# A scatter chain on GpSimd: an expert's output rows are issued when those of the expert one place ahead have landed

## The chip, the cores and the metric

The kernel runs on one core of a Trainium2 chip. The metric is the device time of one execution in microseconds (us), given as the median of several executions. Its engines are named as the profile names them: PE is TensorE (PEld its weight loads), DVE is VectorE, ACT is ScalarE, POOL is GpSimd, SP is SyncE. A DMA is issued by an engine and then moves its bytes on the core's 16 DMA engines; when all 16 have reported, a semaphore has risen by 16 and the DMA has landed.

## The reference

A decoder block on x of shape (16, 256, 256), three parts, each added to the running x after a layer norm: a selective state-space scan, a dynamic time warping alignment with a second input, and a mixture of experts. The change touches only the last one:

```
gate_logits = x @ gate_kernel                      # 4096 tokens, 64 experts
weights, selected = top_k(gate_logits, 2); weights = softmax(weights)
per expert: out = (silu(xe @ w0[e]) * (xe @ w1[e])) @ wo[e]      # 256 -> 512 -> 256
y[token] = sum over its 2 experts of weight * out
```

So each of 4096 tokens has two rows of expert output, 8192 rows of 256 floats (1 KB) in all, and y is their weighted sum.

## The kernel before, in words

The kernel is written in direct instructions, one program for each engine, with semaphores between them. Four stages follow each other: the scan (to about 510 us), the time warping (to about 720 us), the stage `expand` that applies the alignment, makes the normalized tokens `xn`, routes them and clears the DRAM array `outs` to zero (to about 837 us), and the stage `experts` (lines 2130 to 2493), in which everything below happens.

`outs` in DRAM has one row for each (token, choice) pair and after them a region of rows into which unused places of a tile are dumped. `K.table` lists for each place of an expert the token row to fetch, `K.choice` the row of `outs` to write. Experts are ranked by their number of tokens, and each rank has a fixed room: the 32 largest have 220 down to 134 rows ("wide", two tiles of at most 128 rows), the others 128 rows ("narrow", one tile). `TURN` takes 63 ranks alternately, a wide one at even places k and a narrow one at odd k. What doesn't fit in the rooms, and the 64th rank, is worked off afterwards in a loop over "late" tiles whose number is read at run time; with these inputs it runs once.

For each place k in 0..62:

- SP loads the expert's weights (1.5 MB, three DMAs of 512 KB, `load_weights`, issue line 2127) into a ring of 4; the load for place k waits until place k-4 has left the ring (`down_mm`).
- POOL fetches the token rows with indirect DMAs, one per tile (`gather`, line 2221), into `mo_xg`, a ring of XR = 4 buffers. The gather of place k+4 waits until PE has turned the tile of place k (`turned`).
- PE transposes the rows (`turn`, line 2274; DVE copies them to `mo_xt` at line 2411), multiplies with w0 and w1 (`up`, line 2288), ACT takes the silu (line 2370), DVE the product (line 2417), PE multiplies with wo (`down` line 2294 for narrow, `down_wide` line 2302 and the turning back `back` line 2313 for wide ones).
- DVE copies the result to `mo_o`, a ring of XR = 4 buffers (`take_out`, line 2428), and raises `o_ok`. Before it does, it waits for the landing of the scatter four places ahead, which used the same buffer (`o_out[k % XR]`).
- POOL sends the rows to `outs` with indirect DMAs that add to what lies there (`scatter`, line 2228), one per tile; each raises `o_out[k % XR]` by 16 when it has landed. `moved(k)` is the value that this semaphore has once place k and all before it in the same buffer have landed.

POOL's program is written out in this order:

```
for k in range(RANKS):
    if k + XR < RANKS:
        gather(k + XR)
...
    scatter(k)
```

After the 63 places POOL's late loop (from line 2246) scatters the late tile (line 2250, a plain write), fetches the next one and prepares its indices. Then SP waits for all `o_out`, reads `outs` back in 16 DMAs of 512 KB (line 2209), DVE forms the weighted sums (line 2491), and ACT sends them out.

Of the kernel before, what the change touches and what calls it, by code (L numbers as in the profile page):

```python
# [44 lines left out]
RANKS = E - 1  # L45
# [29 lines left out]
def settle(eng):  # L75


    eng.nop(nofuse=True)
# [80 lines left out]
XR = 4  # L159
# [1970 lines left out]
def experts(K):  # L2130
# [3 lines left out]
    with ExitStack() as c:  # L2134
# [25 lines left out]
        o_out = [sem(f"mo_o_out{u}") for u in range(XR)]  # L2160
# [17 lines left out]
        moved = lambda k: sum(16 * len(tiles(j)) for j in range(k % XR, k + 1, XR))  # L2178
# [5 lines left out]
        def late_count(eng):  # L2184
            return eng.value_load(K.late_n[0:1, 0:1], min_val=1, max_val=LATE + 1)  # L2185

        @block.sync
        def _(sp):
            sp.wait_ge(x_in[0], moved(0))
            for k in range(1, WRING):  # L2190
                load_weights(K, sp, expert_at(K, sp, k), k)
            for k in range(WRING, RANKS):
                sp.wait_ge(down_mm, (k - WRING + 1) * FC)
                load_weights(K, sp, expert_at(K, sp, k), k % WRING)
            n = late_count(sp)
            with sp.Fori(0, n) as g:
                e = sp.value_load(K.late_of[0:1, bass.ds(g, 1)], min_val=0, max_val=E - 1)
                sp.wait_ge(done, g + 1)
                settle(sp)
                load_weights(K, sp, e, RANKS % WRING)  # L2200
            for u in range(XR):
                if u != LAST:
                    sp.wait_ge(o_out[u], moved_by(u))
            sp.wait_ge(o_out[LAST], n * 16 + moved_by(LAST))
            settle(sp)
            for k in range(TT // G):
                if k >= GOT:
                    sp.wait_ge(added, (k - GOT + 1) * 2 * G)
                sp.dma_start(got[k % GOT][:, :, :, :],
                             K.outs_dram[2 * k * G * P:2 * (k + 1) * G * P, :].rearrange("(t p i) d -> p t i d", p=P,  # L2210
                                                                                       i=2)
                             ).then_inc(got_in[k % GOT], 16)

        @block.gpsimd
        def _(pool):

            def gather(k):
                if k >= XR:
                    pool.wait_ge(turned, k - XR + 1)
                for a, at, n in tiles(k):  # L2220
                    nc.gpsimd.indirect_dma_start(xg[k % XR][0:n, a, :], None, K.xn_dram[:, :],  # L2221
                                                 bass.IndirectOffsetOnAxis(ap=K.table[0:n, at:at + 1], axis=0)
                                                 ).then_inc(x_in[k % XR], 16)

            def scatter(k):
                pool.wait_ge(o_ok, k + 1)
                for a, at, n in tiles(k):
                    nc.gpsimd.indirect_dma_start(K.outs_dram[:, :],  # L2228
                                                 bass.IndirectOffsetOnAxis(ap=K.choice[0:n, at:at + 1], axis=0),
                                                 o_sb[k % XR][0:n, a, :], None,  # L2230
                                                 compute_op=ALU.add).then_inc(o_out[k % XR], 16)

            for k in range(1, XR):
                gather(k)
# [3 lines that stand above are left out]
                if k + XR == RANKS:  # L2238
                    nc.gpsimd.tensor_copy(to[:, :], K.choice[:, LATE0:LATE0 + 1]).then_inc(indices, 1)
                    pool.wait_ge(turned, RANKS - XR + 1)  # L2240
                    nc.gpsimd.indirect_dma_start(xg[LAST][:, 0, :], None, K.xn_dram[:, :],
                                                 bass.IndirectOffsetOnAxis(ap=K.table[:, LATE0:LATE0 + 1], axis=0)
                                                 ).then_inc(x_in[LAST], 16)
                scatter(k)
            n = late_count(pool)
            with pool.Fori(0, n) as g:
                pool.wait_ge(o_ok, g + RANKS + 1)
                pool.wait_ge(indices, g + 1)
                settle(pool)
                nc.gpsimd.indirect_dma_start(K.outs_dram[:, :], bass.IndirectOffsetOnAxis(ap=to[:, :], axis=0),  # L2250
                                             o_sb[LAST][:, 0, :], None).then_inc(o_out[LAST], 16)
                pool.wait_ge(named_ok, g * 3 + 3)
                settle(pool)
                nc.gpsimd.indirect_dma_start(xg[LAST][:, 0, :], None, K.xn_dram[:, :],
                                             bass.IndirectOffsetOnAxis(ap=index[:, :], axis=0)).then_inc(x_in[LAST], 16)
                pool.wait_ge(x_in[LAST], g * 16 + (moved_by(LAST) + 32))
                pool.wait_ge(o_out[LAST], g * 16 + (moved_by(LAST) + 16))
                settle(pool)
                nc.gpsimd.tensor_copy(to[:, :], to_next[:, :]).then_inc(indices, 1)
            for u in range(XR):  # L2260
                if u != LAST:
                    pool.wait_ge(o_out[u], moved_by(u))
            settle(pool)

        @block.tensor
        def _(pe):
# [40 lines left out]
            def back(k):  # L2307
                pe.wait_ge(ot_ok, backs(k))
                if k >= 2:
                    pe.wait_ge(o_ok, k - 1)  # L2310
                for a, _, n in tiles(k):
                    for c_ in range(DC):
                        m = nc.tensor.transpose(o_ps[k % 2][0:n, a, c_ * P:(c_ + 1) * P],  # L2313
                                                ot[:, c_, a * P:a * P + n], K.ident[:, :])
                m.then_inc(back_mm, 1)
# [89 lines left out]
        def _(dve):  # L2405
# [14 lines left out]
            def take_out(k):  # L2420
                if wide[k]:
                    dve.wait_ge(back_mm, backs(k))
                else:
                    dve.wait_ge(down_mm, k * FC + FC)
                if k >= XR:
                    dve.wait_ge(o_out[k % XR], moved(k - XR))
                for a, _, n in tiles(k):
                    m = nc.vector.tensor_copy(o_sb[k % XR][0:n, a, :], o_ps[k % 2][0:n, a, :])  # L2428
                m.then_inc(o_ok, 1)
# [172 lines left out]
```

## Time and profile before

| | us |
|---|---|
| median of 3 executions | 1307.4 (1305.8 to 1307.7) |
| the profiled execution, its own time | 1307.59 |
| its span, first to last instruction | 1305.8 |
| stage `experts`, first gather to last scatter issue | 837.3 to 1258.4 |
| from there to the end (late tile, read back, sums) | 1258.4 to 1305.8 |
| PE busy in the span | 1036.5 (79%) |
| POOL busy in the span | 695.1 (53%) |

The profiled execution stands 0.2 us above the median, and its span 1.8 us below its own time. The profile consists of a page (busy time by engine, the span cut in 40 slices, DMA queues, the chain that ended last, groups of instructions) and of views of the trace for stretches of it: instructions in order of time, who waited for whom, busy time in a stretch, and DMA traffic by queue in a stretch. Queue q1 is that of SP and carries the weights, q0 is that of POOL and carries gathers and scatters. POOL's "busy" for a DMA is the time in which it writes the descriptors; the bytes move later.

### The profile page before, as it was taken

The numbers are of one execution on the slowest core, as the hardware profiler recorded it, in microseconds if no ns is written. First come the engines' busy times: TensorE is split into PE (matmuls) and PEld (weight loads), VectorE is DVE, ScalarE is ACT, GpSimd is POOL, SyncE is SP. The second block draws the span as 40 slices with busy tenths as digits, with TensorE's granted clock in tenths as the row PEclk, the third lists the DMA queues.
The fourth block names the chain that finished last, engine by engine and source line by source line (L and its number), as shares of the span: only waits on it lengthen the run. The fifth ranks groups of instructions, "written<-read, shape, count | busy, mean of one in ns | idle before, by whom it ended". The sixth has DMA issues, their size and how long they took to land. (4 is left out here: it accounts for less than half of the span.)

```text
span 1305.8 us, 21090 instructions
## 1 busy us (share of the span) xinstructions
PE 1036.5 (79%) x6867; PEld 924.2 (71%) x6867; DVE 927.7 (71%) x2072; ACT 580.2 (44%) x1286; POOL 695.1 (53%) x609
## 2 busy tenths in 40 slices
PE   5767888787878768477746788799999999999970
PEld 4666767686767757466511576599999999999960
DVE  6999999999999996688798599433333333333348
ACT  3768787878778764344340454121221222222210
POOL 4886868788888870200000554346556565655620
PEclk8889989999999999555578899599999999999985
DMA  8644555464646551122203244499999999999939
GB/s 241 191 142 143 162 164 176 135 203 140 190 150 199 158 168 42 26 41 49 41 1 129 89 149 151 167 291 277 267 271 281 292 288 303 295 306 298 278 105 351
DMA packets 177597, 239.82 MB, mean 184 GB/s; under 512 B 33778, under 2 KB 104486, under 8 KB 176848
## 3 DMA queue, kind: packets, MB, share of 16 engines
q1 hardware_dynamic: 153968, 215.06, 52.1%
q0 software_dynamic: 17184, 18.97, 7.0%
q10 hardware_dynamic: 6336, 4.44, 1.1%
q8 instruction: 55, 0.90, 0.3%
q14 instruction: 54, 0.44, 0.1%
HBM read 203.01 MB, written 31.19 MB: 179 GB/s over the span
## 5 line engine op out<-in xcount | busy, mean ns | idle before, releaser
L1010 PE MATMUL st_y_ps<-ident,st_hc 128*128 128x128 f32 x2048 | 273.6, 292 | 113.3 <-DVE st_hc L529 113.2
L1010 PEld LDWEIGHTS st_y_ps<-ident,st_hc 128*128 128x128 f32 x2048 | 255.4, 203 | 135.6 <-DVE st_hc L529 134.7
L412 POOL TENSOR_TENSOR st_u<-st_dx,codes 128x1024 f32<-128x1024 f32 x127 | 296.4, 2361 | 39.2 <-DVE st_h L521 31.4
L521 DVE TENSOR_TENSOR_SCAN st_h<-st_da,st_u 128x512 f32<-128x512 f32 x256 | 297.6, 1203 | 0.2 <-POOL st_u L412 0.2
L2288 PE MATMUL mo_h<-mo_xt,w 128*128 128x128 f32 (+17 forms) x2048 | 282.1, 289 | 2.0 <-DVE mo_xt L2411 2.0
L2288 PEld LDWEIGHTS mo_h<-mo_xt,w 128*128 128x128 f32 x2048 | 271.6, 193 | 6.6 <-issue 2.7
L2417 DVE TENSOR_TENSOR mo_inter<-mo_silu,mo_h 128x128 f32<-128x128 f32 (+17 forms) x256 | 77.8, 304 | 246.2 <-ACT mo_silu L2370 204.3
L2228 POOL DMA_INDIRECT outs<-mo_o,choice x95 | 149.6, 1575 | 149.2 <-DVE mo_o L2428 130.3
L2370 ACT ACTIVATE mo_silu<-mo_h 128x128 f32<-128x128 f32 (+17 forms) x256 | 74.4, 291 | 286.6 <-PE mo_h L2288 198.5
L748 ACT ACTIVATE st_da<-st_delta,st_a_neg 128x510 f32<-128x510 f32 x256 | 172.1, 685 | 58.6 <-DVE st_h L521 54.1
L529 DVE TENSOR_TENSOR st_hc<-st_h,st_cps 128x1024 f32<-128x1024 f32 x128 | 152.5, 1192 | 0.0
L2221 POOL DMA_INDIRECT mo_xg<-xn,table x93 | 92.7, 997 | 33.7 <-issue 28.1
L1294 PE MATMUL wv_e<-wv_r,wv_shift 128*128 128x1 f32 x274 | 75.9, 348 | 40.3 <-DVE wv_r L1232 39.4
L1294 PEld LDWEIGHTS wv_e<-wv_r,wv_shift 128*128 128x128 f32 x274 | 68.5, 312 | 48.0 <-issue 46.0
L755 ACT ACTIVATE st_cps<-codes 128x512 f32<-128x512 f32 x128 | 76.7, 599 | 43.4 <-DVE st_hc L529 42.1
L2302 PE MATMUL mo_ot_ps<-mo_inter,wo 128*128 128x190 f32 (+16 forms) x512 | 84.7, 298 | 0.0
L1652 POOL TENSOR_SCALAR ex_on<-ex_apart,ex_reach 128x256 f32<-128x256 f32 x32 | 30.3, 959 | 97.1 <-ACT ex_apart L1980 97.0
L2294 PE MATMUL mo_o_ps<-wo,mo_inter 128*128 128x256 f32 x256 | 74.2, 393 | 0.4 <-DVE mo_inter L2417 0.4
L2302 PEld LDWEIGHTS mo_ot_ps<-mo_inter,wo 128*128 128x128 f32 x512 | 73.6, 190 | 0.0
L1284 ACT ACTIVATE wv_r<-wv_e,wv_edge_big 128x1 f32<-128x1 f32 x137 | 35.8, 261 | 64.6 <-PE wv_e L1294 64.6
L1363 POOL MEMSET ex_earlier<- 128x128 bf16 x1 | 0.2, 205 | 104.8 <-POOLq L1107 104.8
L1232 DVE TENSOR_TENSOR_SCAN wv_r<-wv_m,wv_r,wave 128x64 f32<-128x64 f32 x136 | 47.8, 352 | 4.8
(394 smaller groups left out, 1472.9 us busy)
## 6 DMA issues: line engine op xcount, KB each, us to landing
codes<-bc SPq DMA_DIRECT2D x256, 256.0 KB, 3.7
w<-in_L_ffn_w_dram SPq DMA_DIRECT2D x128, 512.0 KB
wo<-in_L_ffn_wo_dram SPq DMA_DIRECT2D x64, 512.0 KB
outs<-ex_zero SPq DMA_DIRECT2D x16, 512.0 KB, 3.2
co_got<-outs SPq DMA_DIRECT2D x16, 512.0 KB, 6.0
wave<-dist SPq DMA_DIRECT2D x16, 274.0 KB
x<-in_x_dram SPq DMA_DIRECT2D x8, 512.0 KB, 9.4
st_cx<-in_ctx_dram SPq DMA_DIRECT2D x8, 512.0 KB, 4.0
```

The lines of the kernel that those rows point to most:

```text
L412: nc.gpsimd.tensor_tensor(u_sb[k % URING][:, :, :], dx[p % 2][:, :, :], over_chunks(b_sb[k % BRING]), ALU.mult).then_inc(u_ok, 1)
L521: nc.vector.tensor_tensor_scan(h_sb[k % HRING][:, dh, :], da_ps[dh][:, :], u_sb[k % URING][:, dh, :], 0.0, ALU.mult, ALU.add).then_inc(h_o ...
L529: nc.vector.tensor_tensor(hc_sb[k % RING][:, :, :], h_sb[k % HRING][:, :, :], over_chunks(c_ps[k % 2][:, :]), ALU.mult).then_inc(hc_ok, 1)
L748: nc.scalar.activation(by_batch(da_ps[dh][:, :]), by_batch(delta[p % 2][:, dh, :]), ACT.Exp, scale=a_neg[:, dh, n:n + 1]).then_inc(da_ok, 1)
L755: nc.scalar.activation(c_ps[k % 2][:, :], c_sb[k % CRING], ACT.Copy).then_inc(c_ok, 1)
L1010: m = nc.tensor.matmul(y_ps[t // 2][:, t % 2, dh * P:(dh + 1) * P], hc_sb[k % RING][:, dh, t * P:(t + 1) * P], K.ident[:, :], start=False, ...
L1294: nc.tensor.matmul(e_ps[t % 4][:, 0:1], K.shift[:, :], r[:, t + 1, SW:SW + 1], start=True, stop=True).then_inc(e_mm, 1)
L2221: nc.gpsimd.indirect_dma_start(xg[k % XR][0:n, a, :], None, K.xn_dram[:, :], bass.IndirectOffsetOnAxis(ap=K.table[0:n, at:at + 1], axis=0) ...
L2228: nc.gpsimd.indirect_dma_start(K.outs_dram[:, :], bass.IndirectOffsetOnAxis(ap=K.choice[0:n, at:at + 1], axis=0), o_sb[k % XR][0:n, a, :], ...
L2288: ins = nc.tensor.matmul(h_ps[m][:, i, 0:n], K.w[r][i][:, c_, m * P:(m + 1) * P], xt[u][:, c_, 0:n], start=(c_ == 0), stop=(c_ == DC - 1))
L2302: ins = nc.tensor.matmul(ot_ps[:, c_, 0:n], K.w[r][2][:, m, c_ * P:(c_ + 1) * P], inter[m][:, 0:n], start=(m == 0 and c_ == 0), stop=(m == ...
L2417: nc.vector.tensor_tensor(inter[m][:, 0:n], silu[m][:, 0:n], h_ps[m][:, 1, 0:n], ALU.mult).then_inc(inter_ok, 1)
```

## The change

`scatter(k)` gets a second wait: for k of 1 and more, POOL waits until all tiles of place k-1 have landed, before it issues the tiles of place k. The late loop's scatter waits for the landing of the last place, 62, as well. No instruction, transfer or buffer is added, removed or resized; the order of POOL's instructions stays.

```
             def scatter(k):
                 pool.wait_ge(o_ok, k + 1)
+                if k >= 1:
+                    pool.wait_ge(o_out[(k - 1) % XR], moved(k - 1))
                 for a, at, n in tiles(k):
                     nc.gpsimd.indirect_dma_start(K.outs_dram[:, :],
...
             with pool.Fori(0, n) as g:
                 pool.wait_ge(o_ok, g + RANKS + 1)
                 pool.wait_ge(indices, g + 1)
+                pool.wait_ge(o_out[(RANKS - 1) % XR], moved(RANKS - 1))
                 settle(pool)
```

How POOL's instructions stand, place by place, with the semaphores that each waits for. First the steady part, around places 2 to 4: `mo_xg<-xn` is a gather, `outs<-mo_o` a scatter; of two scatters in a row (a wide place) only the first has waits.

```order
-L2228 DMA outs<-mo_o,choice 40960x256 [waits mo_o_ok]
-L2228 DMA outs<-mo_o,choice 40960x256
-L2221 DMA mo_xg<-xn,table 128x256 [waits mo_turned]
-L2228 DMA outs<-mo_o,choice 40960x256 [waits mo_o_ok]
+L2230 DMA outs<-mo_o,choice 40960x256 [waits mo_o_out1,mo_o_ok]
+L2230 DMA outs<-mo_o,choice 40960x256
+L2221 DMA mo_xg<-xn,table 128x256 [waits mo_turned]
+L2230 DMA outs<-mo_o,choice 40960x256 [waits mo_o_out2,mo_o_ok]
 L2221 DMA mo_xg<-xn,table 128x256 [waits mo_turned]
```

Nothing has moved; the scatter of each place has one wait more, on the buffer of the place ahead. A gather behind a waiting scatter is issued later by as much as that scatter waits.

Then the late loop, at the end of POOL's program:

```order
-L2250 DMA outs<-mo_o,mo_to 40960x256 [waits mo_indices]
-L2252 ISA
-L2254 DMA mo_xg<-xn,mo_index 128x256 [waits mo_named_ok]
+L2253 DMA outs<-mo_o,mo_to 40960x256 [waits mo_indices,mo_o_out2]
+L2255 ISA
+L2257 DMA mo_xg<-xn,mo_index 128x256 [waits mo_named_ok]
```

Here too only a wait has come in, on buffer 2, that of place 62. On the other engines nothing differs but line numbers.

## Rows read from the trace of the kernel before

**Rows 1.** The page: busy time by engine, and the granted clock in 40 slices.
```profile
PE 1036.5 (79%) x6867; PEld 924.2 (71%) x6867; DVE 927.7 (71%) x2072; ACT 580.2 (44%) x1286; POOL 695.1 (53%) x609
PEclk8889989999999999555578899599999999999985
```

**Rows 2.** Busy by stretch: PE, PEld, DVE, ACT, POOL, clock, DMA share, GB/s.
```profile
860.00:900.00 40.00, 40.00 (x275) 38.48 (x274) 12.84 (x37) 8.13 (x25) 22.14 (x17) 1.00 0.90 268
1000.00:1100.00 100.00, 100.00 (x764) 96.11 (x763) 34.34 (x102) 21.15 (x70) 58.92 (x47) 1.00 0.96 294
```

**Rows 3.** Who waited for whom, 860 to 1265 us: total us, times, longest.
```profile
POOL outs L2228 <- DVE mo_o L2428: 121.6, 32, 5.4
```

**Rows 4.** POOL in order of time: start us, us, line, what, idle before it.
```profile
853.61 1.66 POOL L2228 DMA_INDIRECT outs<-mo_o,choice  x1 [8.69 <-DVE mo_o L2428]
868.12 1.63 POOL L2228 DMA_INDIRECT outs<-mo_o,choice  x1 [4.39 <-DVE mo_o L2428]
...
993.39 1.62 POOL L2228 DMA_INDIRECT outs<-mo_o,choice  x1 [4.21 <-DVE mo_o L2428]
998.86 1.60 POOL L2228 DMA_INDIRECT outs<-mo_o,choice  x1 [0.30 <-issue]
...
1006.77 1.62 POOL L2228 DMA_INDIRECT outs<-mo_o,choice  x1 [3.79 <-DVE mo_o L2428]
1008.69 1.86 POOL L2228 DMA_INDIRECT outs<-mo_o,choice  x1 [0.30 <-issue]
1010.86 1.03 POOL L2221 DMA_INDIRECT mo_xg<-xn,table  x1 [0.30 <-issue]
1012.20 1.60 POOL L2228 DMA_INDIRECT outs<-mo_o,choice  x1 [0.30 <-issue]
...
1019.90 1.62 POOL L2228 DMA_INDIRECT outs<-mo_o,choice  x1 [3.58 <-DVE mo_o L2428]
1024.84 1.61 POOL L2228 DMA_INDIRECT outs<-mo_o,choice  x1 [0.30 <-issue]
...
1146.54 1.63 POOL L2228 DMA_INDIRECT outs<-mo_o,choice  x1 [3.37 <-DVE mo_o L2428]
1151.53 1.60 POOL L2228 DMA_INDIRECT outs<-mo_o,choice  x1 [0.30 <-issue]
1158.94 1.62 POOL L2228 DMA_INDIRECT outs<-mo_o,choice  x1 [3.29 <-DVE mo_o L2428]
```

**Rows 5.** The scatters of line 2228 in the whole span: ns min/median/max, then landing.
```profile
L2228 POOL DMA_INDIRECT outs<-mo_o,choice x95: 1331/1605/2202, 853.6 to 1257.0; - x95
DMA to landing us min/median/max: 3.7/7.0/8.2
```

**Rows 6.** Landing of the scatters that start from 860 to 1230 us.
```profile
DMA to landing us min/median/max: 6.1/7.0/8.2
```

**Rows 7.** Landing of the scatter that starts at 998.86 us.
```profile
DMA to landing us min/median/max: 6.7/6.7/6.7
```

**Rows 8.** Landing of the scatter that starts at 1024.84 us.
```profile
DMA to landing us min/median/max: 7.2/7.2/7.2
```

**Rows 9.** DMA by queue (packets, MB, share), 1146.5 to 1149.3 us, all of it.
```profile
q1 hardware_dynamic: 699, 1.04, 104.0%
```

**Rows 10.** DMA by queue, 1149.3 to 1151.5 us.
```profile
q0 software_dynamic: 176, 0.15, 47.3%
```

**Rows 11.** DMA by queue, 1151.5 to 1156.3 us.
```profile
q0 software_dynamic: 48, 0.13, 7.0%
```

**Rows 12.** PE in order of time, the turning of place 27's rows.
```profile
1028.20 0.38 PE L2274 MATMUL mo_xt_ps<-ident,mo_xg 128*128 128x128 f32 x2
```

**Rows 13.** POOL in order of time, the end of the stage.
```profile
1255.14 1.56 POOL L2228 DMA_INDIRECT outs<-mo_o,choice  x1 [5.42 <-DVE mo_o L2428]
1257.00 1.37 POOL L2228 DMA_INDIRECT outs<-mo_o,choice  x1 [0.30 <-issue]
1265.71 1.02 POOL L2250 DMA_INDIRECT outs<-mo_o,mo_to  x1 [7.34 <-DVE mo_o L2482]
```

More of the change, by code:

```diff
@@ L2226, in scatter @@
                 pool.wait_ge(o_ok, k + 1)
+                if k >= 1:
+                    pool.wait_ge(o_out[(k - 1) % XR], moved(k - 1))
                 for a, at, n in tiles(k):
@@ L2248, in _ @@
                 pool.wait_ge(indices, g + 1)
+                pool.wait_ge(o_out[(RANKS - 1) % XR], moved(RANKS - 1))
                 settle(pool)
```

## The prediction

> **What bounds the kernel now.** I read the busy time of the page first [rows 1]: PE 79% and DVE 71% of the span, POOL 53%, so over the whole span no engine is full. The change lies in the stage `experts` alone, so the busy time by stretch comes next [rows 2]: from 860 to 900 us PE is busy 40.00 of 40.00 us, from 1000 to 1100 us 100.00 of 100.00, each time at granted clock 1.00, which is the 2.4 GHz level. The stage goes at PE's pace, and nothing that the DMAs or POOL do there can make it shorter. The DMA engines are nearly full too (share 0.90 to 0.96), with q1, the weights, in front. The view of who waited for whom [rows 3] says how POOL stands: 121.6 us in 32 waits of line 2228, all for DVE's `mo_o`. These are the 31 wide places behind the first, and one narrow place near the end: POOL runs ahead of PE and waits for each wide result; the narrow one behind it goes out as soon as POOL is through, 0.30 us after a gather.
>
> So the question is one of rhythm. POOL in order of time [rows 4] gives it: wide scatters start at 853.61 and 868.12, at 1006.77 and 1019.90, at 1146.54 and 1158.94, and the last at 1255.14 [rows 13]. A pair of places takes 14.5 us at first, 13.1 in the middle, 12.4 in the last third, and (1255.14 - 853.61) / 31 = 12.95 on the mean.
>
> **The change, part by part.** It adds waits and nothing else. POOL's issue time stays: 95 scatters of 1.6 us [rows 5]. What is new is that a pair now holds two landings one behind the other.
>
> *The narrow one's wait for the wide one.* Before, it starts 1151.53 - 1146.54 = 5.0 us behind the wide scatter's first issue, in other pairs 5.4 to 5.5 (998.86 - 993.39, 1012.20 - 1006.77) [rows 4]. When has the wide one landed? The landing column shows values of 3.7 to 8.2 us from issue, median 7.0 [rows 5], and between 860 and 1230 us 6.1 to 8.2 [rows 6]; I take these as narrow places' values, since two tiles share a semaphore at a wide one. For wide ones I bound it: at least 1.9 us to the second issue (1008.69 - 1006.77) plus 3.7, so 5.6; at most 1.9 + 8.2 = 10.1. The traffic of q0 says where in between. Place 44 (142 rows, 0.15 MB) is issued at 1146.54; up to 1149.3 the only queue with traffic is q1 [rows 9], then q0 moves 0.15 MB up to 1151.5 [rows 10]. All of its bytes are there 5.0 us after the first issue, so I take the lower end, 5.6, and the narrow one's start moves by about 0.6 + 0.3 for the reaction (0.30 us is what POOL leaves between any two issues). It delays nothing behind it on POOL by itself but the next two gathers.
>
> The Trainium skill would price a landing far lower: its page "DMA: Bandwidth & Descriptors", section "Anatomy of one DMA", fits 2.0 us plus bytes / 436e3, so 2.3 us for a tile of 131 KB, and by it every wait added here would be met before POOL asks, with the same sum of zero. No row bears that out: 3.7 is the least, 7.0 the median [rows 5].
>
> *The wide one's wait for the narrow one.* Place 25 starts at 1024.84, 4.94 us behind its wide scatter, and lands 7.2 us later [rows 8], so 12.1 behind it. Place 21 starts 5.47 behind its own and lands after 6.7 [rows 7], so 12.2 behind it. Half a microsecond of later issue gives no later landing. I read it so: the narrow rows wait for the weight load that is under way and go out when it ends, whichever of the two moments they were issued in. So a delay of up to a microsecond is swallowed, and the pair's chain takes 12.15 + 0.3 = 12.45 us. Against the rhythm that is 2.1 us to spare early, 0.7 in the middle, 0.5 on the mean, and none (-0.05) in the last third: over its 8 or so pairs the lag grows to 0.4 us. A pair that lands late is made good in the following ones.
>
> *What a lag costs.* PE doesn't see a late scatter, it sees a late gather, which is queued behind it on POOL. The gather of place 27 is issued at 1010.86 [rows 4]; with 7.0 us to land (the traffic of such a gather, 0.13 MB, is over 6.1 us after its issue at 1150.2 [rows 11]) it is there at 1017.9, and PE turns its rows at 1028.20 [rows 12]. That is 10.3 us of cover. The ring of `mo_o` covers more: DVE refills a buffer four places later, about 25 us after its issue, against 5.6 to 10.1 us to land. So lags under 10.3 us cost nothing. If that cover were gone, each further microsecond of lag would be one of the run.
>
> *The late loop.* Its scatter waits for place 62, issued last at 1257.00; with 8.2 us that lands at 1265.2, before the late scatter's 1265.71 [rows 13]. Nothing.
>
> *Sum.* 0 on the profiled execution's 1307.6, which stands 0.2 above the median of 1307.4. A measurement of this kernel can't tell less than about 0.2% (2.6 us) from no change.
>
> **The rivals.**
>
> A. *The chain is stacked and outlasts PE* (slower). If a landing follows its own issue by the same time whenever it is issued, the narrow one's delay is not swallowed. The pair then takes 5.6 + 0.3 + 7.0 + 0.3 = 13.2 us, and with one wide scatter in three landing 1 to 2 us later (the values of 8.2 show that there are such) about 13.6. That is 0.65 over the mean rhythm, 31 x 0.65 = 20 us of lag, 10.3 of it covered: +10, or 1318. It decides from a pair of 12.95 + 10.3 / 31 = 13.3 us on. The far end, wide 1.9 + 7.0 and narrow 7.0, gives 16.5 and (16.5 - 12.95) x 31 - 10 = +100 us; the traffic of [rows 10] speaks against it. For A speaks that only two pairs carry my reading, and that they differ by 0.5 us. The Trainium skill speaks for A too: on the same page, "Queues, rings and completion order", an engine takes turns between its queues packet by packet, so that q0 would not have to wait for a load's end. The 2.8 us with q1 alone [rows 9] neither prove nor refute it, as descriptors are being written for part of them.
>
> B. *Missed gaps* (slower). If rows really move only in the gap between two weight loads, a late landing misses the next gap and costs a place, 12.95 / 2 = 6.5 us. The cover holds one and a half of them; four misses in the stage give 4 x 6.5 - 10.3 = +16, or 1323. This needs a lag that isn't made up in between.
>
> C. *The added waits never bite* (no change). If a wide scatter has landed 5.0 us after its issue, as its last bytes in [rows 10] allow, each wait is met when POOL comes to it, and the trace is that of before. Same time as the forecast.
>
> D. *Faster.* With fewer transfers at once the weights could come sooner, but PE is full at clock 1.00 [rows 2] and takes nothing from it. Only chance is left here.
>
> **How the numbers follow.** Forecast (waits bite, the lag stays under the cover) 0.47, C 0.08, A 0.30, B 0.10, D 0.05. So slower 0.40, the same 0.55, faster 0.05; the likeliest is 1307.6. The two cases without a change hold 1305 to 1310 among them. The range goes down to 1304.5 for the spread of the runs, and up through A (1318) and B's 1323 to 1326, which leaves out A's far half and part of D.
>
> **What would show it.** In the new profile the stage's busy time of PE should again be 100 of 100 us at 1.00. POOL's waits should change their names: those for DVE at wide places remain, about as many, and beside them stand waits of about 1 us for a DMA on `outs` before most narrow scatters, 31 of them, some 30 us in all. Landings should stay near 7 us or fall a little. The first gather of place 5 and its like should start within 10 us of their old distance to PE. The forecast is wrong if PE has waits for `mo_xg` at its turning, if wide scatters stop waiting for DVE and wait for a DMA at nearly every place from some point on, or if a pair's distance on POOL is over 13.3 us in the middle of the stage. It is right by luck if POOL waits for DMAs at every place and PE still doesn't stall.

## The result and the profile after

The changed kernel takes 1338.5 us, the median of four executions (1335.6 to 1344.3), against 1307.2 before: 1.0244 times as long, with an interval of 1.0225 to 1.0262. Measured again in a later session it took 1342.9 (ratio 1.0256, 1.0218 to 1.0294). Its executions lie 9 to 11 us apart, where those of the kernel before lie within 2 to 4. The profiled execution is the longest of the first four, 1344.3 us with a span of 1342.5, so the sums below stand against the profiled execution of before: 1344.3 - 1307.6 = 36.7 us. One execution each of the kernels earlier_again (3521 us) and plain_no_chain (2943 us), both described below, took more than twice as long as the others and is left out of their medians.

The page of the profile after, with the engines' busy time, the granted clock in slices, and the head of the chain that ended last (by engine, then by line):

```profile
PE 1043.2 (78%) x6867; PEld 925.3 (69%) x6867; DVE 927.9 (69%) x2072; ACT 580.2 (43%) x1286; POOL 695.3 (52%) x609
...
PEclk8899999999999998555768996999998999998985
...
DMA 16%; PE 12%; POOL 4%; issue 3%; DVE 2%; ACT 0%; DVEq 0%; POOLq 0%; ACTq 0%; SPq 0%
DMA outs<-mo_o,choice 12%; PE mo_h L2291 7%; POOL outs L2230 3%; DMA mo_xg<-xn,table 3%; PE mo_ot_ps L2305 2%; DMA co_got<-outs 2%; PE mo_o_ps L2297 2%; DVE x L2494 1%; PE mo_xt_ps L2277 1%; POOL mo_xg L2221 1%; DVE mo_o L2431 0%; PE mo_o_ps L2316 0%; DVE mo_marks L2478 0%; DMA outs<-mo_o,mo_to 0%; PE mo_ot_ps L2360 0%
```

Every engine has as many instructions as in [rows 1]; PE is busy 6.7 us longer (1043.2 against 1036.5), DVE, ACT and POOL within 0.2 us of before. The chain that ended last has changed hands: 16% of the span are DMA, 12% that of the adding scatters, and 12% are PE, where before it was 32% PE and 2% DMA. In the last third of the slices the granted clock falls below full at places where PE now has pauses (0.97 and 0.98 in the rows below).

The busy time by stretch, columns as in [rows 2]:

```profile
860.00:900.00 40.00, 40.00 (x276) 38.47 (x275) 12.93 (x37) 8.13 (x25) 19.11 (x14) 1.00 0.87 263
900.00:950.00 50.00, 50.00 (x351) 48.49 (x350) 15.74 (x45) 10.38 (x32) 24.80 (x19) 1.00 0.90 267
1000.00:1100.00 100.00, 93.86 (x690) 89.26 (x689) 30.96 (x92) 19.22 (x63) 52.53 (x41) 0.97 0.87 259
1100.00:1200.00 100.00, 91.42 (x699) 86.10 (x698) 30.67 (x93) 19.10 (x64) 54.26 (x44) 0.98 0.89 264
```

Up to 950 us PE is as full as before. From 1000 us on it lacks 6 to 9 us in 100 (the first pauses, 3.1 us in all, lie between 950 and 1000), and the DMA engines have become less busy (0.87 against 0.96 from 1000 to 1100 us), not more. So neither PE's work nor a full set of DMA engines holds the stage. Who waited for whom, 837 to 1300 us, says what:

```profile
POOL outs L2230 <- DMA outs<-mo_o,choice: 125.3, 44, 6.0
...
POOL outs L2230 <- issue: 33.3, 40, 5.9
POOL outs L2230 <- DVE mo_o L2431: 32.3, 10, 8.6
PEld mo_xt_ps L2277 <- DMA mo_xg<-xn,table: 28.8, 14, 4.7
...
PE mo_xt_ps L2277 <- DMA mo_xg<-xn,table: 24.4, 13, 4.3
```

The 121.6 us that POOL waited for DVE [rows 3] have become 32.3, and 125.3 us are waits for the landing of another scatter, at wide and narrow places alike. PE waits 13 times for gathered rows, which it never did before. POOL in order of time, two stretches, columns as in [rows 4]:

```profile
853.51 1.66 POOL L2230 DMA_INDIRECT outs<-mo_o,choice  x1 [8.63 <-DVE mo_o L2431]
...
864.84 1.60 POOL L2230 DMA_INDIRECT outs<-mo_o,choice  x1 [6.04 <-DMA outs<-mo_o,choice]
...
872.18 1.63 POOL L2230 DMA_INDIRECT outs<-mo_o,choice  x1 [2.82 <-DVE mo_o L2431]
...
1089.19 1.60 POOL L2230 DMA_INDIRECT outs<-mo_o,choice  x1 [1.66 <-DMA outs<-mo_o,choice]
1091.10 1.00 POOL L2221 DMA_INDIRECT mo_xg<-xn,table  x1 [0.30 <-issue]
1092.40 0.92 POOL L2221 DMA_INDIRECT mo_xg<-xn,table  x1 [0.30 <-issue]
1097.07 1.63 POOL L2230 DMA_INDIRECT outs<-mo_o,choice  x1 [3.75 <-DVE mo_o L2431]
...
1105.06 1.62 POOL L2230 DMA_INDIRECT outs<-mo_o,choice  x1 [3.31 <-DMA outs<-mo_o,choice]
```

From the narrow scatter at 1089.19 to the wide one it is 7.9 us, from that to the next narrow one 8.0: 15.9 for a pair that took 12.6 in this part of the stage before. It is one of the long ones; from place 22 to place 42 a pair takes 14.3 us on the mean (12.7 before). Already at the first narrow place the start has moved from 5.6 us behind the wide one to 11.3. The name `DVE mo_o` in the row at 1097.07 is one of those that a wait for two semaphores can bring: the landing before it was the later of the two.

The end of the stage:

```profile
1297.00 1.76 POOL L2230 DMA_INDIRECT outs<-mo_o,choice  x1 [3.04 <-DMA outs<-mo_o,choice]
1299.07 1.37 POOL L2230 DMA_INDIRECT outs<-mo_o,choice  x1 [0.31 <-DVE mo_o L2485]
1302.50 1.02 POOL L2253 DMA_INDIRECT outs<-mo_o,mo_to  x1 [2.06 <-ACT mo_to_next L2399]
```

The last place's scatter starts at 1297.00 instead of 1255.14 [rows 13], 41.9 us later. From there to the end of the span it is 45.5 us instead of 50.7: the late tile's arithmetic is already done, and its scatter follows 5.5 us behind the last place's instead of 10.6. 41.9 - 5.2 = 36.7 us, which is the whole loss of the profiled execution. A pair takes (1297.00 - 853.51) / 31 = 14.31 us where it took 12.95.

The starts of all 63 places and the trace's landing events (the rises of a place's semaphore) split this pair. From a wide to the next narrow start it is 7.9 us on the mean (before 5.05), from a narrow to the next wide 6.4 (before 7.9). 54 of 62 scatters start 0.73 to 0.78 us after the last landing event of the one ahead; this is called the reaction from here on. By the same events a wide place lands 7.0 us after its first issue (6.2 before) and a narrow one 5.6 after its own (7.0 before). 7.0 + 5.6 + 2 x 0.75 = 14.1, within 0.2 of the pair. Events are missing in each trace, and where the last one of a place is missing its landing reads too short: of the 32 wide places of the kernel before only 2 have all their events, so 6.2 is a lower bound.

### The profile page after: what moved, and what is told of

Its sections match the earlier page's. It is cut to its first block and busy times, and to the rows that moved or that the text cites. A ratio compares the mean times of both kernels' runs of the same rounds, so it can differ in the third digit from the quotient of the medians.

```text
span 1342.5 us, 21152 instructions
## 1 busy us (share of the span) xinstructions
PE 1043.2 (78%) x6867; PEld 925.3 (69%) x6867; DVE 927.9 (69%) x2072; ACT 580.2 (43%) x1286; POOL 695.3 (52%) x609
## 5 line engine op out<-in xcount | busy, mean ns | idle before, releaser
L2291 PEld LDWEIGHTS mo_h<-mo_xt,w 128*128 128x128 f32 x2048 | 274.9, 195 | 7.0 <-issue 2.8
L2230 POOL DMA_INDIRECT outs<-mo_o,choice x95 | 149.8, 1577 | 191.1 <-DMA outs<-mo_o,choice 125.3
L2297 PE MATMUL mo_o_ps<-wo,mo_inter 128*128 128x256 f32 x256 | 76.9, 405 | 0.4 <-DVE mo_inter L2420 0.4
L2414 DVE COPY mo_xt<-mo_xt_ps 128x380 f32<-128x380 f32 (+16 forms) x64 | 29.2, 457 | 46.2 <-PE mo_xt_ps L2277 43.3
L2277 PE MATMUL mo_xt_ps<-ident,mo_xg 128*128 128x128 f32 (+16 forms) x192 | 33.7, 269 | 29.2 <-DMA mo_xg<-xn,table 24.4
```

Source lines behind the costliest of these rows:

```text
L2291: ins = nc.tensor.matmul(h_ps[m][:, i, 0:n], K.w[r][i][:, c_, m * P:(m + 1) * P], xt[u][:, c_, 0:n], start=(c_ == 0), stop=(c_ == DC - 1))
L2297: nc.tensor.matmul(o_ps[k % 2 if isinstance(k, int) else RANKS % 2][0:n, 0, :], inter[m][:, 0:n], K.w[r][2][:, m, :], start=(m == 0), stop ...
```

## The experiments

Theory one, after this reading: two landings and two reactions in a row outlast PE's pair, and the chain sets the pace from the second place on. The rivals that the experiments set against it are named two to five, in the order in which they come up. Each kernel below was timed in rounds beside the kernel before (medians of 1307.3 to 1308.2 in these sessions).

**One link at a time.** Two kernels hold only half of the chain. A third holds one wait for each place from 2 on, 61 in all, but each is for the place two ahead, so that two shorter chains run side by side. The first cut shows the line of each of the two halves; a kernel has one of them.

```
                pool.wait_ge(o_ok, k + 1)
-                if k >= 1:
+                if k % 2 == 1:                     # narrow_waits
+                if k >= 1 and k % 2 == 0:          # wide_waits
                     pool.wait_ge(o_out[(k - 1) % XR], moved(k - 1))
```

```
-                if k >= 1:
-                    pool.wait_ge(o_out[(k - 1) % XR], moved(k - 1))
+                if k >= 2:                         # two_apart
+                    pool.wait_ge(o_out[(k - 2) % XR], moved(k - 2))
```

All three are without the wait in the late loop.

> Only the narrow places wait for the landing of the wide one ahead; the wide ones and the late loop are as before. Theory one (two landings and two reactions in a row, 7.0 + 0.75 + 5.6 + 0.75 = 14.1 us, outlast PE's pair of 12.95): with one link cut the pair's chain is 7.0 + 0.75 and fits, so 1307 to 1309 us, and wide scatters wait for DVE again. Rival two (each added wait holds up the gathers behind it by itself, and the loss of 31 us is the sum of single waits): the narrow waits, the longer ones against the old order, bring half or more of it, 1323 us or over.

> Only the wide places wait for the landing of the narrow one ahead. Theory one: the narrow one starts 5 us behind the wide one and lands 12.1 behind it, with 0.75 for the reaction 12.9, against a pair of 14.5 to 12.1 us: near balance, a small lag in the last third that the cover of 10 us takes, so 1307 to 1312 us. Rival two: up to half of the loss, about 1320.

> Each place waits for the landing two places ahead, so two chains run side by side, with as many waits as in the change. Theory one: a wide scatter and its reaction take 7.75 us of the 12.95 of a pair, a narrow one 6.4, both fit, 1307 to 1309 us. Rival two: the same number of waits costs a similar time, 1320 or over.

Measured: 1311.0 us with the narrow places' waits (ratio 1.0026, 1.0017 to 1.0036), 1308.5 with the wide places' (1.0003, 0.9994 to 1.0013), 1308.0 two places apart (0.9997, 0.9988 to 1.0007). Rival two, single waits that add up, falls: 61 waits two apart cost nothing that can be told from zero, and the two halves of the chain together 3 us, not 31. Theory one missed narrow_waits by 2 us, and its second forecast, that wide scatters would wait for DVE again, failed there. POOL in order of time in narrow_waits:

```profile
1064.28 1.62 POOL L2230 DMA_INDIRECT outs<-mo_o,choice  x1 [0.30 <-issue]
1066.21 1.41 POOL L2230 DMA_INDIRECT outs<-mo_o,choice  x1 [0.31 <-issue]
1067.93 1.05 POOL L2221 DMA_INDIRECT mo_xg<-xn,table  x1 [0.30 <-PE mo_xt_ps L2276]
1072.66 1.60 POOL L2230 DMA_INDIRECT outs<-mo_o,choice  x1 [3.68 <-DMA outs<-mo_o,choice]
1074.56 1.00 POOL L2221 DMA_INDIRECT mo_xg<-xn,table  x1 [0.30 <-issue]
1075.86 0.91 POOL L2221 DMA_INDIRECT mo_xg<-xn,table  x1 [0.30 <-issue]
1077.08 1.63 POOL L2230 DMA_INDIRECT outs<-mo_o,choice  x1 [0.30 <-issue]
```

The wide scatter is issued 0.30 us after a gather, for POOL comes to it late; 8.4 us on follows the narrow one, and 4.4 us of POOL's own issuing later the next wide one. That is 12.8, against a pair of 12.6 there in the kernel before. The wide landing has grown: 7.8 us on the mean in the landing events, against 6.2 before. That isn't the work of the missing events alone: in the DMA packets of queue q0, the middle one of the 1 KB packets within 8.5 us of a wide place's first issue ends after 5.25 us, against 3.81 before (means over places 12 to 58), 1.4 us later. The rows sent are the same, but two things differ: the moment within the weight loads, and that two gathers now stand directly ahead on the same queue, issued 1.2 and 2.5 us earlier (4.6 and 5.9 before). So a landing's length depends on when its scatter is issued and on what goes ahead of it; no run separates the two.

**What makes the landings long: the weight traffic.** In two kernels each weight load of places 4 to 62 brings one block of 128 by 128 instead of 512 KB, so these experts compute with old weights.

```
     for w, dram in zip(K.w[r], (K.w0_dram, K.w1_dram, K.wo_dram)):
-        sp.dma_start(w[:, :, :], one(dram)).then_inc(K.w_in[r], 16)
+        if light:
+            w, src = w[:, 0:1, 0:P], one(dram)[:, 0:1, 0:P]
+        else:
+            w, src = w[:, :, :], one(dram)
+        sp.dma_start(w, src).then_inc(K.w_in[r], 16)
...
-                load_weights(K, sp, expert_at(K, sp, k), k % WRING)
+                load_weights(K, sp, expert_at(K, sp, k), k % WRING, True)
```

> Leaves out most of the weight loads: for places 4 to 62 each of the three loads brings one block of 128 by 128 instead of 512 KB, so these experts work with old weights. The whole chain stays. Theory one (landings are long because of the weight traffic): landings fall to those seen without it, 5.6 us for a wide and 3.7 for a narrow place, the pair's chain to 10.8 us with the reactions, under PE's 12.95: 1306 to 1309 us. Rival four (the waits and their reaction hold up POOL's gathers whatever the traffic): 1325 us or over.

> Its partner without the chain: the same reduced weight loads in the kernel before. PE was full, so 1306 to 1308 us by every theory.

Measured: 1308.1 us with the chain (1.0002, 0.9992 to 1.0011) and 1307.0 without it (1.0001, 0.9992 to 1.0011). The full chain costs 1.0 us or nothing as soon as most of the weight traffic is gone. The landing events give 5.4 us for wide and 3.6 for narrow places, so 10.5 with both reactions, under 12.95; many events are missing here, and both are lower bounds. Rival four falls.

**Or the adding.** The same chain with plain writes for the 63 places:

```
-                                                 o_sb[k % XR][0:n, a, :], None,
-                                                 compute_op=ALU.add).then_inc(o_out[k % XR], 16)
+                                                 o_sb[k % XR][0:n, a, :], None).then_inc(o_out[k % XR], 16)
```

> The whole chain as in the change, but the scatters of the 63 places write their rows plainly instead of adding. If the adding is what makes landings long (the old row must be read first), they fall by about 1 us each, the pair's chain from 14.3 to some 12.5 us, and the time to 1308 us. If the weight traffic is the cause, landings and time stay, 1335 to 1340 us.

Measured: 1308.4 us (1.0012, 1.0002 to 1.0022), on the first branch of what was expected. The line of the scatters from the view of one line (count, then ns of one issue, min/median/max), and PE from 1000 to 1100 us:

```profile
L2230 POOL DMA_INDIRECT outs<-mo_o,choice x95: 863/993/1300, 852.7 to 1255.5; - x95
```

```profile
1000.00:1100.00 100.00, 100.00 (x764) 96.11 (x764) 34.05 (x101) 21.12 (x70) 45.44 (x48) 1.00 0.86 290
```

A plain scatter takes POOL 1.0 us to issue instead of 1.6 [rows 5], and lands 5.3 us (wide) and 5.0 us (narrow) after its issue in the landing events. The pair's chain is then 11.8 us, and PE is full again. The two causes aren't alternatives: taking away either the weight traffic or the adding brings the chain under PE's pair.

**Is PE out of the bound?** Two kernels leave out a part of PE's work.

```
             def up(k, r, u, m, n):
...
+                half = 1 if isinstance(k, int) and m >= 2 else DC
                 for i in range(2):
-                    for c_ in range(DC):
+                    for c_ in range(half):
...
-                                               xt[u][:, c_, 0:n], start=(c_ == 0), stop=(c_ == DC - 1))
+                                               xt[u][:, c_, 0:n], start=(c_ == 0), stop=(c_ == half - 1))
```

> Leaves out a part of PE's work: in places 0 to 62 the second half of the contraction of w0 and w1 for the last two of four blocks, some 2.3 us of a pair's 12.95. The whole chain stays. Theory one (the chain alone sets the pace, PE waits for it): nearly nothing is gained, 1320 to 1340 us. Rival five (the stage's time is PE's time plus a fixed loss for stalls): 31 x 2.3 = 71 us less than the change, 1267 us.

> Its partner without the chain, the same part of PE's work left out of the kernel before. PE sets the pace there, so 71 us less, some 1237 us, or somewhat more if the weight loads become the bound.

Measured: 1339.7 us with the chain (1.0239, 1.0207 to 1.0271), 1245.2 without it (0.9530, 0.9514 to 0.9546), where some 1237 was expected. The same work left out is worth 62 us to the kernel before and nothing to the changed one. The time of the changed kernel is that of its chain. PE's waits in chain_less_pe, 837 to 1300 us, and its busy time from 900 to 1250 us:

```profile
PEld mo_xt_ps L2277 <- DMA mo_xg<-xn,table: 68.5, 25, 5.5
PE mo_xt_ps L2277 <- DMA mo_xg<-xn,table: 60.5, 22, 5.3
```

```profile
900.00:1250.00 350.00, 300.27 (x2013) 279.59 (x2013) 106.70 (x320) 67.14 (x221) 188.70 (x148) 0.90 0.88 260
```

PE's 24.4 us of waits for gathered rows have grown to 60.5, which is a good half of the 62. The granted clock has fallen as well, to 0.90 from 900 to 1250 us where the changed kernel has 0.98 with PE busy 326.87 of 350 us, so another part of what was saved went into slower matmuls. Rival five falls.

**Does the cover help?** POOL's gathers were put one place ahead, with the chain and without.

```
-            for k in range(1, XR):
+            for k in range(1, XR + 1):
                 gather(k)
             for k in range(RANKS):
-                if k + XR < RANKS:
-                    gather(k + XR)
+                if k + XR + 1 < RANKS:
+                    gather(k + XR + 1)
```

> The whole chain as in the change, but POOL issues each gather one place earlier, ahead of one more scatter. Theory one in its strict form: the time is the chain's own length, the 42 us by which the last scatter starts later, so nothing is gained, 1335 to 1340 us. Rival three (the loss is the lag less the cover of the gathers, as the prediction had it): one place more of cover, 6.5 us, is gained, 1332 us.

Measured: 1353.9 us (1.0355, 1.0338 to 1.0373). No expectation had this; the changed kernel was not in the same session, so it was repeated beside it.

> The changed kernel once more, beside its variant with earlier gathers. If the chain's pace is a property of the program, 1335 to 1342 us; if it depends on the chip or session, it can come out near the 1354 of the variant.

> The chain with each gather one place earlier, again. If the gap of 15 us was chip and session, this equals chain_again within 3 us. If the order of gathers changes the landings (in the profile a pair took 14.57 us against 14.31), it is 8 to 15 us above chain_again.

> Each gather one place earlier in the kernel before, no chain. By the theory that only the chain's landings count, PE hides everything, 1306 to 1309 us. If the earlier gathers hold up scatters by themselves (a gather waits for PE's turning and the scatter is behind it), 1310 us or over.

Measured in one session: the changed kernel 1342.9 us, with earlier gathers 1351.5 (1.0338, 1.0317 to 1.0358), earlier gathers without the chain 1311.8 (1.0038, 1.0023 to 1.0052). So the gap is real but 9 us, not 15. Earlier gathers cost 4.5 us even without a chain, against theory one's 1306 to 1309, and why they do wasn't looked into. With the chain the pair has grown: between the profiles of chain_again and earlier_again from 14.26 to 14.40 us, so 31 x 0.14 = 4 us for a difference of 3.6 between the profiled executions, and between those of the change and gathers_earlier from 14.31 to 14.57, 8 us for 7.9. Rival three, in which cover is deducted from the lag, asked for a gain. None came, and the longer pair alone accounts for the difference. This variant's profile also shows, for one narrow scatter, the landing and then the reaction. The scatter starts at 1122.66:

```profile
DMA to landing us min/median/max: 6.1/6.1/6.1
```

```profile
1122.66 1.62 POOL L2230 DMA_INDIRECT outs<-mo_o,choice  x1 [0.70 <-issue]
...
1129.52 1.59 POOL L2230 DMA_INDIRECT outs<-mo_o,choice  x1 [3.92 <-DVE mo_o L2431]
```

Landed at 1122.66 + 6.1 = 1128.8, next issue at 1129.52, so 0.7 to 0.8 us between them.

**A part of the chain.** In one kernel only places 1 to 20 wait for the one ahead (`if 1 <= k <= 20:`, no wait in the late loop), in another places 42 to 62 and the late loop (`if k >= 42:`).

> Only places 1 to 20 wait for the one ahead. In the change the scatter of place 20 starts 14.8 us later than before. Theory one with a lag that PE is covered against by 10.3 us: PE loses the 4 to 5 us beyond the cover and the rest of the lag is made good afterwards, 1311 to 1313 us. Rival (every microsecond of the chain's lag is paid, covered or not): 1322 us.

> Only places 42 to 62 and the late loop wait for the one ahead. In the change these 20 places take 128.7 us from scatter to scatter, before 121.0. Theory one with the lag left at the end: 7.7 us of lag stay under the gathers' cover, but the last scatter is late by as much and the late tile's scatter waits for it, with some 6 us of room there before: 1308 to 1311 us. Rival (only lag beyond the gathers' cover costs): 1307 to 1308.

Measured: 1311.4 us (1.0033, 1.0022 to 1.0043) and 1311.9 us (1.0038, 1.0019 to 1.0058). The first is what the theory said, that PE pays what exceeds the cover and the rest of the lag is made good over the following 40 places; in its profiled execution, the longest of eight with 1316.0 us, PE pauses for 6.1 us between 900 and 1250. The second lies 0.9 us above what was expected, and 4 us above the rival, by which only a lag beyond the cover of the gathers costs. Its end of the stage:

```profile
1267.84 2.46 POOL L2230 DMA_INDIRECT outs<-mo_o,choice  x1 [2.88 <-DMA outs<-mo_o,choice]
1270.61 1.37 POOL L2230 DMA_INDIRECT outs<-mo_o,choice  x1 [0.30 <-DVE mo_o L2485]
1274.18 1.02 POOL L2253 DMA_INDIRECT outs<-mo_o,mo_to  x1 [2.21 <-ACT mo_to_next L2399]
```

The last place is 12.7 us late (1255.14 before [rows 13]) and the late tile's scatter 8.5 (1265.71 before [rows 13]). The lag was expected at 7.7 us; it went beyond the cover of 10.3, and PE pauses for 3.1 us in all from 1130 to 1250 us. But this execution took 8.2 us more than the profiled one of before (1315.8 against 1307.6), which is the delay of the late tile's scatter and not the 2.4 us beyond the cover. So the cover is worth something only if there are places left in which to make up for the lag.

**Plain writes without the chain**, the control to chain_plain_write:

> The 63 places' rows are written plainly, no chain. PE sets the pace, so no gain from shorter landings: 1306 to 1308 us. If the adding scatters' traffic had cost PE or the end of the run something, up to 3 us less.

Measured: 1345.9 us (1.0296, 1.0276 to 1.0317), 37.5 us above the same kernel with the chain (in another session), where 1306 to 1308 was expected. PE from 1100 to 1200 us and ACT from 1113 us:

```profile
1100.00:1200.00 100.00, 90.15 (x698) 85.36 (x698) 29.65 (x92) 17.91 (x64) 41.24 (x44) 1.00 0.80 263
```

```profile
1113.56 0.29 ACT L2369 ACTIVATE mo_silu<-mo_h 128x146 f32<-128x146 f32 x1 [2.90 <-PE mo_h L2287]
1117.18 0.29 ACT L2369 ACTIVATE mo_silu<-mo_h 128x146 f32<-128x146 f32 x1 [3.33 <-PE mo_h L2287]
```

PE's matmuls for the second of these end at about 1114.3 us in the trace (such ends are modelled), yet ACT starts 2.9 us later. ACT isn't late by itself: the event with which PE raises the semaphore stands at 1117.16, 0.02 us before ACT's start. In the trace 69 silus of 256 start over 0.8 us after PE's matmul, all of them at wide places, up to 3.8 us and some 155 us in all, part of which overlaps; 41 of them found ACT idle, and each of these starts within 0.06 us of such an event of PE. In the kernel before and in the change there is no late silu, in chain_plain_write there are 7, none over 1.3 us. Around the rows shown POOL issues a plain scatter and two gathers in a row (1113.09 to 1116.5). What holds PE's semaphore back, and why plain writes without the chain do this and adding ones don't, stays open. The control therefore doesn't show what the adding costs without a chain, and chain_plain_write stands on the measured landings alone.

## Why the prediction was wrong

The forecast was no change at 1307.6 us with a range up to 1326; measured is 1338.5. Two steps of it failed: the length of the pair's chain, 12.45 us in the sum and 14.3 in the run, and the deduction of 10.3 us of cover from the lag. All three signs that it had named for being wrong are in the new profile: PE's waits for `mo_xg`, wide scatters that wait for a DMA, and a pair of over 13.3 us in the middle of the stage (14.3).

- *PE bounds the stage, and POOL waits for DVE at wide places.* Right for the kernel before; less_pe confirms it with 62 us.
- *The reaction of 0.3 us.* Wrong. It was taken from POOL's distance between two issues with no wait in between. After a landing POOL takes 0.75 us. In the sum only one reaction in each pair counted, the other was to be swallowed; with 0.75 there the pair is 12.9 and the 0.5 us to spare are all but gone. If both count it is 0.9 us more, 13.35, a lag of 12 us over 31 pairs. So this step took away the margin, but doesn't explain 31 us by itself.
- *The wide place lands 5.6 us after its first issue.* Mis-sized. That was the lower bound, chosen from one place late in the stage where the second tile is short. It is 7.0 in the changed kernel, 1.4 more, 43 us over the stage. Part of it was there before: by thirds of the stage the events give 7.5, 6.0 and 5.4 us in the old trace, lower bounds, so that 5.6 fits the last third only. Part came in when the scatters left their old moments (8.0, 6.7 and 6.4 in the changed kernel), as narrow_waits shows by itself (7.8).
- *A delay of the narrow place is swallowed.* Right in direction: it landed 5.6 us after its issue instead of 7.0. But the reading stood on two pairs whose starts differ by half a microsecond, and the real delay was 2.9 us. In the sum the narrow place starts 5.6 + 0.3 = 5.9 us behind the wide one, lands 6.25 later, and 0.3 on the next wide one starts: 12.45. Measured on the mean are 7.9, 5.7 and 0.75: 14.3.
- *10.3 us of cover.* The size was about right, if low: PE first waits for gathered rows at 976.5 us, where the scatters start 14 to 16 us late. The use was wrong. The sum deducted the cover from the lag as if the lag vanished at the end of the stage. The run ends with a read of everything that was scattered, so a lag at the last place is paid, less the 5.2 us of late work that moved under it. The profiled loss is 41.9 - 5.2, chain_less_pe shows that less work for PE brings nothing back, and the earlier gathers brought no gain either. PE's pauses are the effect here, not the cause.
- *The late loop's wait.* It was never run alone. In the changed profile the late tile's scatter follows the landing of place 62, on which the end of the run depends anyway.
- *Rival A* named the mechanism, from a pair of 13.3 us on, with 1318 at a pair of 13.6. With the measured 14.31 its formula gives 31 x (14.31 - 12.95) - 10.3 = 32 us for a loss of 36.7 in that execution and 31 in the median; for the median it is close by luck, since it deducts a cover that isn't given back and the profiled execution is the longest. *Rival B*, the missed gap, wasn't tested by itself; landings that grow with the moment of issue speak for something of its kind. *Rival C*, waits that never bite, is refuted by 125.3 us of waits. *Rival D*, faster, didn't happen.
- *The estimate of 2.3 us for a landing*, worked out from the fit in the Trainium skill ("DMA: Bandwidth & Descriptors", section "Anatomy of one DMA"), was set aside rightly: even with little weight traffic a narrow adding scatter takes 3.6 us or more from its issue, with it 5.6 to 7.0. By this estimate no wait would have bitten.
- *Turns between queues*, which the Trainium skill states ("DMA: Bandwidth & Descriptors", section "Queues, rings and completion order"), can't be decided here. The weight traffic does lengthen landings, by up to 2.0 us for a narrow place in a chain (5.6 against 3.6, a lower bound), but no run separates taking turns from waiting for a load's end.

What would have shown the danger in the old profile: its landing events give 6.2 us for a wide and 7.0 for a narrow place, 13.2 together against PE's 12.95, before any reaction is added. A balance that close should have been a forecast of slower.

## What to carry to other kernels

A wait for the last transfer's landing before the next issue turns a throughput of transfers into a sum of latencies; compare landing plus reaction, with a reaction taken from a wait for a DMA, with the time the bounding engine needs for the same unit of work, and keep a margin, because landings change with the moment of issue. Where the order that is needed allows it, let two chains run side by side: the wait two places back cost nothing here. Slack in a ring hides a lag only until the end: a lag in what must be complete before the last stage is paid there, less what other work moves under it (5.2 of 41.9 us here).

## What the runs showed of the hardware

- The time from a landing's last event to the next DMA issue on POOL was 0.73 to 0.78 us in 54 of 62 places, against 0.30 between issues without such a wait.
- A landing is as late as the last of its DMA engines. At the 13 wide places of the changed kernel with all 32 events (16 for each of two tiles), 28 of them have come after 6.3 us on the mean, the last after 7.0.
- The same narrow adding scatter of 128 rows of 1 KB lands after 3.6 us (a lower bound) with little weight traffic, 5.6 in a full chain with all of it, 7.0 in the kernel before, where it is issued directly behind a gather. As a plain write in the chain it takes POOL 1.0 us to issue instead of 1.6, and lands after 5.0.
- With plain scatters and no chain the run was 3% longer, and ACT instructions started up to 3.8 us after the matmul they wait for, right behind a late semaphore event of PE; with the chain this all but vanished. Not explained.
- The executions of the chained kernel spread over 9 to 11 us, those of the kernel before over 2 to 4 (the cause wasn't looked into).
